# First attention: Q projected by halves through the transposes' bank in steps 3 and 5, three tiles turned by VectorE, five of eight ratios by ScalarE

## The reference, cut to what matters

```python
Q = einsum('bse,hec->bhsc', X, Wq) + bq      # c = 128: Q1 | Q2
K = einsum('bse,hec->bhsc', X, Wk) + bk      # c = 128: K1 | K2
V = einsum('bse,hed->bhsd', X, Wv) + bv      # d = 64
A1 = Q1 @ K1.T / sqrt(64)
A2 = Q2 @ K2.T / sqrt(64)
P = softmax(A1) - lam * softmax(A2)
O = P @ V
Y = concat_heads(O) @ Wo + bo
Y = layernorm(Y) * gamma + beta, times 0.2;  x = x + Y
```

## Time and profile before

| | us |
|---|---|
| median of 3 runs (lowest, highest) | 1575.7 (1573.21, 1578.5) |
| the profiled execution's own time | 1573.77 |
| its span in the profile | 1572.0 |
| first attention, first to last swap of Q (issues of L490) | 18.7 to 1003.5 |
| PE, DVE, ACT, POOL busy over the span | 92%, 88%, 76%, 64% |

### The profile page before, as it was taken

One profiled execution on the slowest core, in us unless ns is written; L12 is line 12 of the kernel. 1 busy time (PEld: TensorE's weight loads), 2 busy tenths in 40 slices (PEclk: granted clock), 3 DMA queues, 4 the chain that ended last, 5 costly groups with the idle time before them and its releaser, 6 DMA issues.

```text
span 1572.0 us, 28031 instructions
## 1 busy us (share of the span) xinstructions
PE 1439.6 (92%) x10243; PEld 588.5 (37%) x10243; DVE 1376.4 (88%) x2107; ACT 1198.3 (76%) x1911; POOL 1003.8 (64%) x727
## 2 busy tenths in 40 slices
PE   5899999999999999999999999986685999999985
PEld 1434443344434443344334433434541222222223
DVE  6798998999899989999999989988687999999947
ACT  4787888888888888888888888874342888888882
POOL 2999998898898988989889889880032011111112
PEclk9999999999999999999999999997696999999997
DMA  4243433343244323433343333420000110000001
GB/s 126 76 105 92 106 86 82 102 112 90 78 103 110 96 77 104 109 92 85 91 107 105 83 91 93 114 68 1 1 22 21 31 35 15 16 16 16 16 16 34
DMA packets 154641, 110.80 MB, mean 70 GB/s; under 512 B 31381, under 2 KB 142906, under 8 KB 154506
## 3 DMA queue, kind: packets, MB, share of 16 engines
q1 hardware_dynamic: 154378, 108.99, 26.5%
q0 software_dynamic: 128, 0.03, 0.0%
HBM read 53.82 MB, written 34.87 MB: 56 GB/s over the span
## 4 chain that ended last, share of the span: by engine, by line
PE 53%; ACT 14%; DVE 13%; issue 11%; POOL 7%; DMA 1%; SPq 0%; POOLq 0%; ACTq 0%; DVEq 0%
PE PS L1573 14%; PE PS L1585 10%; PE PS L1599 9%; ACT ering L847 7%; PE PS L1980 4%; POOL ering L656 3%; DVE nmx L1152 2%; PE PS L1942 2%; DVE region L1172 2%; PE PS L1632 2%; PE PS L1964 2%; ACT region L871 2%; DVE mxp L1479 2%; ACT ering L1059 2%; POOL ering L655 2%
## 5 line engine op out<-in xcount | busy, mean ns | idle before, releaser
L1152 DVE TENSOR_REDUCE nmx<-PS 128x1 f32<-128x1024 f32 x512 | 620.1, 1216 | 54.4 <-PE PS L1574 53.5
L847 ACT ACTIVATE ering<-PS,nmx 128x1024 f32<-128x1024 f32 x512 | 570.6, 1116 | 109.6 <-DVE nmx L1152 109.5
L656 POOL TENSOR_TENSOR ering<-ering 128x1024 f32<-128x1024 f32 x256 | 604.2, 2360 | 21.4
L1573 PE MATMUL PS<-region 64*128 64x512 f16 x1536 | 405.1, 381 | 20.4 <-ACT ering L847 14.5
L1574 PE MATMUL PS<-region 64*128 64x512 f16 x1536 | 405.2, 381 | 0.0
L655 POOL TENSOR_SCALAR ering<-ering,rho 128x1024 f32<-128x1024 f32 x256 | 287.3, 1122 | 95.2 <-DVE rho L1161 94.5
L1479 DVE TENSOR_REDUCE mxp<-PS 128x2 f32<-128x1024 f32 x256 | 304.2, 1222 | 34.3 <-PE PS L1964 29.9
L1059 ACT ACTIVATE ering<-PS 128x1024 f32<-128x1024 f32 x256 | 259.6, 1024 | 70.0 <-PE PS L1942 64.1
L1585 PE MATMUL PS<-ident,ering 128*128 128x128 f32 x1536 | 251.5, 286 | 15.6 <-ACT t L858 8.1
L1585 PEld LDWEIGHTS PS<-ident,ering 128*128 128x128 f32 x1536 | 161.6, 141 | 201.7 <-issue 73.8
L1573 PEld LDWEIGHTS PS<-region 64*128 64x128 f16 x1536 | 112.6, 94 | 261.3 <-ACT ering L847 110.2
(11 more groups left out here) (301 smaller groups left out, 1876.2 us busy)
## 6 DMA issues: line engine op xcount, KB each, us to landing
ptd<-t SPq DMA_DIRECT2D x256, 128.0 KB, 2.4
region<-region SPq DMA_DIRECT2D x64, 256.0 KB, 3.5
t<-ptd SPq DMA_DIRECT2D x44, 256.0 KB, 3.5
region<-ptd SPq DMA_DIRECT2D x44, 256.0 KB, 3.5
va<-ptd SPq DMA_DIRECT2D x20, 256.0 KB, 3.4
acc<-ptd SPq DMA_DIRECT2D x20, 256.0 KB, 3.5
osb<-scr SPq DMA_DIRECT2D x32, 128.0 KB, 3.3
rcp<-scr SPq DMA_DIRECT2D x32, 128.0 KB, 3.3
```

The source lines that it names most:

```text
L656: P.tensor_tensor(e1, e1, e2, ALU.subtract).then_inc(s_sub_ok, 1)
L847: A.activation((E1, E2)[p][s % 4], PS[:, bank:bank + 2, :].rearrange("p a b -> p (a b)"), ACT.Exp, bias=nmx[:, 2 * s + p:2 * s + p + 1], s ...
L1152: V.tensor_reduce(nmx[:, 2 * s + p:2 * s + p + 1], PS[:, bank:bank + 2, :].rearrange("p a b -> p (a b)"), AX.X, ALU.max, negate=True).then ...
L1573: MM(PS[:, bank, :], top[0:64, ql, q], KT[b][0:64, p, kl, :], start=(j == 0), stop=(j == 2))
```

## The change

The Q of iteration n + 1 leaves the ring of bank pairs and goes through `TRB`, the transposes' bank, one half of 512 columns at a time: the first half is projected in step 3 after `scores(n, 3, 1)`, the second in step 5 after the values; ACT copies the high parts at the ends of steps 3 and 5; DVE makes the low parts in steps 4 and 6, after the step's first maximum. The second half waits until the first has been read, and tile 3's first turn waits until the second has been read. The ring then has 17 users, so the pairs rotate from iteration to iteration (`turn_of`, `y_pair`), and the fills of steps 2 and 3 lose their tighter waits.

`BY_DVE` becomes (0, 1, 2): tile 1 is turned by DVE at the end of step 4, with four more stores and two more loads on SP. Two DRAM tensors and two staging tiles are now shared in turn by three tiles. SP's swap of Q comes after the third tile's stores and ahead of its load. For tiles 2, 3, 4, 6 and 7 the ratio without lam is made by ACT behind the step's first exponent, and POOL multiplies lam in as its second scalar. The two copies and the two subtractions of `part_w` are joined into one each. The values' pieces move: 4 to step 4. In step 6, tile 3's turn comes behind the values.

```diff
+        wqk_s = sb("wqk_s", [128, 2, 128])
+        wq_s, wk_s = wqk_s[:, 0, :], wqk_s[:, 1, :]
...
-        BY_DVE = (0, 2)
+        BY_DVE = (0, 1, 2)
+        BY_ACT = (2, 3, 4, 6, 7)
...
-        def ring(v):
-            at = v + (1 if v >= 1 else 0) + (1 if v >= 5 else 0)
-            return 2 * (at % 3)
-        Y_PAIR, Q_PAIR = 2, 0
+        def turn_of(n, v):
+            return 17 * n + v + (1 if v >= 1 else 0)
+        def ring(n, v):
+            return 2 * (turn_of(n, v) % 3)
+        def y_pair(m):
+            return 2 * ((turn_of(m + 2, 1) - 1) % 3) if m + 2 < last0 else 2
+        def q_done(m, i):
+            return 2 * m + i if m else 1
+        def q_place(m, i):
+            if m == 0:
+                return PS[:, 0:2, :].rearrange("p a b -> p (a b)"), slice(0, T)
+            return TRB, slice(HF * i, HF * i + HF)
...
             def store_blocks(n, i):
-                sp.wait_ge(s_bt_ok, 2 * n + i + 1)
-                if n >= 1:
-                    sp.wait_ge(s_ptr_dma[(n - 1) % 2], 64 * ((n - 1) // 2 + 1))
+                c = len(BY_DVE) * n + i
+                sp.wait_ge(s_bt_ok, c + 1)
+                if c >= 2:
+                    sp.wait_ge(s_ptr_dma[c % 2], 32 * (c // 2))
...
             def load_turned(n, i):
-                sp.wait_ge(s_ptw_dma, 64 * (2 * n + i + 1))
+                c = len(BY_DVE) * n + i
+                sp.wait_ge(s_ptw_dma, 64 * (c + 1))
...
             def swap_q(m):
-                sp.wait_ge(s_qlo_ok, m + 1)
+                sp.wait_ge(s_qlo_ok, 2 * m + 1)
...
-                if n + 1 < last0:
-                    swap_q(n + 1)
+                if n == -1:
+                    swap_q(0)
...
                     load_turned(n, 0)
                     store_blocks(n, 1)
                     load_turned(n, 1)
+                    store_blocks(n, 2)
+                    if n + 1 < last0:
+                        swap_q(n + 1)
+                    load_turned(n, 2)
...
             def subtract(n, s):
-                link(P.tensor_scalar(e2, e2, rho[:, s:s + 1], 1.0, ALU.mult, ALU.mult))
+                link(P.tensor_scalar(e2, e2, rho[:, s:s + 1], cols[:, LAM:LAM + 1] if s in BY_ACT else 1.0, ALU.mult,
+                                     ALU.mult))
...
+            def ratio(n, s):
+                act.wait_ge(s_rr_ok, 8 * n + s + 1)
+                if s > 0 or n > 0:
+                    act.wait_ge(s_rho_ok, 8 * n + s)
+                A.activation(rho[:, s:s + 1], sums[:, s, 0:1], ACT.Identity, scale=rr[:, n % 2, 1, s:s + 1],
+                             bias=0.0).then_inc(s_rho_ok, 1)
...
                     if own:
                         exponent(n, s, 0)
+                    if (own if s else prv) and (s + 7) % 8 in BY_ACT:
+                        ratio(n if s else n - 1, (s + 7) % 8)
                     if later and (s + 5) % 8 in BY_PE:
                         keep_t(m, (s + 5) % 8, 1)
-                    if s == 2 and nxt and own:
-                        high_q(n + 1)
                     if own:
                         exponent(n, s, 1)
+                    if s in (3, 5) and nxt and own:
+                        high_q(n + 1, (3, 5).index(s))
...
                     if own:
                         maximum(n, s, 0)
+                    if s in (4, 6) and nxt and own:
+                        low_q(n + 1, (4, 6).index(s))
...
-                    if s == 2 and nxt and own:
-                        low_q(n + 1)
-                    if own and s in (3, 5):
-                        turn_blocks(n, s // 2 - 1)
+                    if own and s - 3 in BY_DVE:
+                        turn_blocks(n, BY_DVE.index(s - 3))
...
             def scores(n, s, p):
                 if v == 3 and n >= 2:
                     pe.wait_ge(s_y_ok, n - 1)
-                elif v == 7 and n + 1 < last0:
-                    pe.wait_ge(s_qlo_ok, n + 2)
-                elif v in (1, 2, 5, 6):
+                elif v in (1, 2):
                     at_least(pe, s_exp, u - 1)
                 else:
                     at_least(pe, s_exp, u - 2)
...
             def turn(n, s, i):
                 at_least(pe, s_tr_ev, turned(n, s) + i)
+                if (s, i) == (BY_PE[0], 0) and n + 1 < last0:
+                    pe.wait_ge(s_qlo_ok, 2 * (n + 1) + 1)
...
-            PIECES = {3: (0, 1, 2), 4: (3,), 5: (4, 5, 6), 6: (7,)}
+            PIECES = {3: (0, 1, 2), 4: (3, 4), 5: (5, 6), 6: (7,)}
...
-                    if own and s >= 4:
+                    if own and s >= 3:
                         scores(n, s, 1)
-                    if later and (s + 5) % 8 in BY_PE:
+                    if later and s != 6 and (s + 5) % 8 in BY_PE:
                         turn(m, (s + 5) % 8, 0)
-                    if s == 2 and nxt and own:
-                        project_q(n + 1)
+                    if s == 3 and nxt and own:
+                        project_q(n + 1, 0)
...
                         for j in PIECES[s]:
                             values(n - 1, j)
+                    if s == 5 and nxt and own:
+                        project_q(n + 1, 1)
+                    if s == 6 and later:
+                        turn(m, 3, 0)
```

More of the change, by code:

```diff
@@ L147, in two_layers @@
         iota = xs[:, :, :].rearrange("p l t -> p (l t)").bitcast(F32)
-        wqh, wkh = [r16(15360 + 256 * i, 256).rearrange("p (l c) -> p l c", l=2) for i in range(2)]
+        wqkh = r16(15360, 512).rearrange("p (i l c) -> p i l c", i=2, l=2)
+        wqh, wkh = wqkh[:, 0, :, :], wqkh[:, 1, :, :]
         G2 = eflat[:, 4096:8192].rearrange("p (k n) -> p k n", n=N)
@@ L637, in part_w @@
                 pool.wait_ge(s_k0_mm, 4 * h)
[L638 to L641, removed]
+                link(P.tensor_copy(wqkh[:, :, 0, :], wqk_s[:, :, :]))
+                P.tensor_tensor(wqkh[:, :, 1, :], wqk_s[:, :, :], wqkh[:, :, 0, :], ALU.subtract).then_inc(s_wlo_ok, 1)
             def part_x(i):
@@ L719, in _ @@
             scale_q(0)
+            pool.wait_ge(s_ld_l0, 48)
             for n in range(last0):
@@ L843, in exponent @@
                     if tile in BY_DVE:
-                        act.wait_ge(s_bt_ok, 2 * prev + BY_DVE.index(tile) + 1)
+                        at_least(act, s_bt_ok, len(BY_DVE) * prev + BY_DVE.index(tile) + 1 if prev >= 0 else 0)
                     else:
@@ L854, in keep_t @@
                 act.wait_ge(s_tr_mm, turned(n, s) + i + 1)
-                if s in (1, 4) and i == 0:
+                if s in (3, 4) and i == 0:
                     at_least(act, s_pv_mm, n - 1 + half)
@@ L866, in high_k, with high_q @@
                              bias=bqk[:, m // 2, 1 + part:2 + part]).then_inc(s_khi_ok, 1)
-            def high_q(m):
-                act.wait_ge(s_q_mm, m + 1)
+            def high_q(m, i):
+                src, at = q_place(m, i)
+                act.wait_ge(s_q_mm, q_done(m, i))
                 at_least(act, s_fill, 16 * (m - 1))
-                A.activation(QT[m % 2][:, 0, :], PS[:, Q_PAIR:Q_PAIR + 2, :].rearrange("p a b -> p (a b)"),
-                             ACT.Identity, bias=bqk[:, m // 2, 0:1]).then_inc(s_qhi_ok, 1)
+                A.activation(QT[m % 2][:, 0, at], src, ACT.Identity, bias=bqk[:, m // 2, 0:1]).then_inc(s_qhi_ok, 1)
             for n in range(-1, last0 + 1):
@@ L1159, in weigh @@
                 V.reciprocal(rr[:, b, :, s], sums[:, s, :]).then_inc(s_rr_ok, 1)
+                if s in BY_ACT:
+                    return
                 dve.wait_ge(s_rr_ok, q + 1)
@@ L1168, in low_k, with low_q @@
                                        in1=KT[m % 2][:, part, 0, :], op0=ALU.add, op1=ALU.subtract).then_inc(s_klo_ok, 1)
[L1170 to L1174, removed]
+            def low_q(m, i):
+                src, at = q_place(m, i)
+                dve.wait_ge(s_qhi_ok, q_done(m, i))
+                V.scalar_tensor_tensor(out=QT[m % 2][:, 1, at], in0=src, scalar=bqk[:, m // 2, 0:1],
+                                       in1=QT[m % 2][:, 0, at], op0=ALU.add, op1=ALU.subtract).then_inc(s_qlo_ok, 1)
             def normalise(n):
@@ L1241, in _ @@
                         dve.wait_ge(s_bias_ev, 1)
-                        low_q(0)
+                        low_q(0, 0)
                         low_k(0, 0)
@@ L1593, in values @@
                 if j == 0:
-                    pe.wait_ge(s_ptr_dma[n % 2], 64 * (n // 2 + 1))
+                    c = len(BY_DVE) * n + len(BY_DVE) - 1
+                    for i in range(2):
+                        pe.wait_ge(s_ptr_dma[i], 32 * ((c - i) // 2 + 1))
                 if j % 4 == 0:
@@ L1612, in to_out, with project_q @@
                     r = slice(64 * half, 64 * half + 64)
-                    mm = MM(PS[:, Y_PAIR + half, :], wo_s[r, :], on[r, :], start=True, stop=True)
+                    mm = MM(PS[:, y_pair(n) + half, :], wo_s[r, :], on[r, :], start=True, stop=True)
                 mm.then_inc(s_y_mm, 1)
-            def project_q(m):
+            def project_q(m, i):
```

(14 more changed lines are left out.)

37 lines of the change are left out of this document (18 added, 19 removed).

## The result

The changed kernel takes 1780.64 us (median of 4 runs, 1777.27 to 1781.84) against 1575.63 us; the ratio is 1.1297, 95% interval 1.1272 to 1.1321. The forecast was 1680 us, in a range of 1600 to 1730: slower was right, and the time lies 50 us above the range. The span of the profiled execution went from 1572.0 to 1775.5 us, by 203.5.

A forecast was written before the change was run, and what follows sets the result against it. Four engines were busy within 5 us of each other in a 31.77 us iteration; the late swap's chain on SP would set 35.3. 30 × 3.6 = +108, less 1, on 1573.8 gave 1681, rounded to 1680 us, range 1600 to 1730.

The forecast's parts named there:

- The chain from tile 3's reciprocal over SP's queue to the landed swap: SP's serial stores, loads and swap delay the next first fill to 35.3 us, +3.6 an iteration; chance 0.62.
- the term of the chain's start, 19.3 us: On DVE, tile 3's reciprocal starts 19.3 us after the iteration's first fill, before 20.0.
- the half clock apart as a rival at 0.12: PE's clock halves behind each swap wait, adding 1.5 to 2 us an iteration: 1725 to 1740 us; chance 0.12.
- the wait that I reckoned, 2.6 us: PE idle ahead of each iteration's first fill, from 32.7 to 35.3 us, until the swap lands.
- the upper bound, +5.2: Chain ends at 37.0 us if the reciprocal stays at 20.0 and the swap queues 1 us behind tile 2's stores.
- the chain itself, 16.0 us: SP's way from tile 3's reciprocal at 19.3 us to the landed swap and next fill at 35.3: 16.0 us.
- the microsecond that I allowed for transfers queued behind each other: In the upper bound only, the swap queues 1 us behind tile 2's four stores.
- the forecast's 35.3: Time from one iteration's first fill to the next, set by SP's chain: 35.3 us against 31.77.
- if loads were all: Work added and removed on the engines, without waits, would make the iteration about 1.2 us shorter.
- The faster rival: Swap lands before PE asks, so 1.2 us an iteration are won: -37, 1537 us; chance 0.11.
- The second rival: DVE's order before tile 3's first turn sets the next fill at 32.7 us, +0.9: 1602 us; chance 0.10.
- the 1 us named: PE waits near 1 us before tile 3's first turn, ended by DVE's low part of Q.

The follow-up runs named there:

- moved up in the changed kernel: The changed kernel with SP's swap of Q issued behind tile 1's stores, ahead of tile 1's loads and tile 2's stores: 1594.49 us, ratio 1.0121.
- the best order found: Changed kernel with swap ahead of tile 1's loads, Q's second half earlier, tile 3's second turn behind step 7's first fill: 1567.81 us, ratio 0.9962.

## Why the prediction was right in its mechanism, and where its size was wrong

**Right: the mechanism.** The chain from tile 3's reciprocal over SP's queue to the landed swap sets the pace; the moved line alone, put into the kernel before, costs 221 us, and moved up in the changed kernel it gives back 186 of 205. The order on SP, the stores of tile 1 right behind tile 0's loads, the wait of the first fill ended by the DMA and 10 half turns are all in the trace as forecast. The first fills stand 38.6 us apart instead of 35, and PE's wait is 4.3 us instead of 2 to 3. Two terms of the sum were too small, each by some 50 us of the total.

**Mis-sized: the term of the chain's start, 19.3 us.** It was worked out at full clock. I had set the half clock apart as a rival at 0.12, because the wait that I reckoned, 2.6 us, was half of the one seen at the program's start. It was not a rival but a part of the same case. The clock fell behind 29 of the 30 waits, which were 4.3 us on average, and the start came at 21.0 us. With PE kept busy it came at 19.35. The price that I put on the rival, 1.5 to 2 us an iteration, was right, with 1.7 measured; its chance was wrong, and so was the choice between all iterations and none. With the swap between tile 1's loads and tile 2's stores, 19 waits lie between 2.3 and 3.0 us, around my 2.6, and 8 of them are followed by half clock and 11 are not. So even the wait that I reckoned would have cost a part of the price, and the longer wait that came cost nearly all of it. As a term of the same sum, 1.7 us would have made the forecast 1730, and the upper bound, +5.2 with it, 1780.

**Mis-sized: the chain itself, 16.0 us.** It took 17.6 us on average, and 17.3 in the iteration shown. From tile 1's stores to its loads 5.0 us pass on average instead of 4.08 (5.30 in the iteration shown, 551.64 to 556.94), between the swap's two issues 0.8 instead of 0.53, from the second to the fill 4.3 instead of 3.91, and 0.4 goes between the groups of loads and stores; the reciprocals' round was shorter, 1.6 instead of 2.03. The stores landed after 2.9 us in the median where they took 2.4 before. So the microsecond that I allowed for transfers queued behind each other, as a bound and on the swap alone, was due, and most of it on the stores. Why the stores take longer to land was not tried by itself.

**The sum.** From the first fill of n = 1 to that of n = 31, 64.10 to 1221.25, 30 iterations took 38.6 us each. Before, 62.39 to 1020.11, they took 31.9. That makes 199 of the 203.5 us between the spans; the first iteration and the end hold the rest. Against the forecast's 35.3 it is 3.27 us more: 1.71 for the start and 1.56 for the chain. Times 30 that is 98 us, and 1681 and 98 are 1779, where the profiled execution took 1777.3. With only one of the two missing, the time would have stood near 1730, at the end of the range.

**The loads.** The 1.2 us by which the iteration would be shorter "if loads were all" were PE's load. ACT's ratios took 0.28 us each where I had 0.20, and POOL's multiplications 0.08 more than nothing. Experiments with single parts show that DVE and POOL count as much: the third tile alone cost 10 us, the ratios alone 15. The faster rival was thus worth less than its 37 us even with a swap in time: the best order found wins 7 us. Q's halves, the rotated bank pairs and the joined weight operations were not tried by themselves.

**The second rival** was right as a mechanism and near in size: 1602 forecast for it, 1594 measured once the swap was out of the way. In the changed kernel its sign is there too, smaller than the 1 us named: PE waits 0.68 us for DVE's low half ahead of tile 3's first turn in the iteration shown.

## What to carry to other kernels

When a transfer is moved within a queue, add up everything that the queue waits for ahead of it, and read from that sum when it lands; the engine that needs it may be three stages away. If the sum says that TensorE will stand still in every iteration, a lower clock behind the wait belongs in the same sum, not in a case of its own: here waits of 2.8 us on average lowered it in 17 of 30 iterations and waits of 4.3 us in 29. Work taken from one of four evenly loaded engines gained nothing here until its receiver, and the engine that waits for the receiver, had room.

## What the runs showed of the hardware

- Clock: behind the waits for the swap, 2.4 to 5.6 us, the granted clock fell to 0.5 in 29 of the 30 iterations n = 1 to 30; behind one of 2.68 us (n = 2) it stayed at 1.00. Over the first 5.5 us it was 0.51 behind the wait of 5.10 us and 0.69 behind that of 4.20, although PE had been busy for 26.97 of the 29.70 us ahead of the latter (531.90 to 561.60). The Trainium skill, TensorE: Matmul & The Clock Gate, Part 1, has the clock halved by idleness; the trace agrees, with 0.51.
- 16 pairs of matmuls that compute nothing, put into that wait, kept the clock at 1.00 in 29 of 30 iterations and took 44 us off the kernel.
- The second of the swap's two transfers landed after 3.9 us in the median behind stores, and after 4.9 us behind loads (two kernels), with 3.7 us in the kernel before, where SP had issued nothing for over 8 us ahead of all but the first. That the loads are the cause was not tried by itself.
- POOL's multiplication of 128 x 1024 by a scalar from memory and a constant took 1.12 us, by two scalars from memory 1.20 us. ACT's ratio of 128 x 1 took 0.28 us.
